# Last four attention units: heads and denominators placed from SBUF to SBUF, without the DRAM buffer

## The reference, cut to what matters

```python
q, k, v = (split_heads(holo_linear(x, ...)) for each of q, k, v)
attn = softmax(einsum('bhqd,bhkd->bhqk', q, k) * scale)
out = einsum('bhqk,bhkd->bhqd', attn, v)          # then back to [B, L, C]
x = _layernorm(x + holo_linear(out, basis_o, phase_o, amp_o))
logits = x @ router_w                              # the router of the experts
```

## Time and profile before

| | |
|---|---|
| median of 3 runs | 962.42 us (960.38 to 962.68) |
| the profiled execution, its own time | 961.26 us |
| its span in the profile | 959.6 us |
| PE busy | 757.4 us (79%) |
| DVE busy | 742.0 us (77%) |
| ACT busy | 470.8 us (49%) |
| mean granted clock of TensorE | 0.925 |

### The profile page before, as it was taken

How to read it: one execution, slowest core, us unless ns; L and a number is a source line. 1 busy time by engine, 2 the same in 40 slices (tenths; PEclk the granted TensorE clock), 3 DMA queues, 4 the chain that set the end, 5 groups by cost and what they waited for, 6 DMA issues and landing times.

```text
span 959.6 us, 12348 instructions
## 1 busy us (share of the span) xinstructions
PE 757.4 (79%) x3664; PEld 301.3 (31%) x3664; DVE 742.0 (77%) x1187; ACT 470.8 (49%) x550; POOL 395.6 (41%) x511
## 2 busy tenths in 40 slices
PE   5369999999999999988669983964667766678783
PEld 3212222222222222245547771321222222225211
DVE  3589999999999999666011225878999999998758
ACT  2237777777777777734213222784323323231452
POOL 3526533322333222005714543008987787570000
PEclk9659999999999999997979996956999989899997
DMA  5652122212222113120124413023544434420131
GB/s 125 203 210 53 53 54 56 53 49 53 55 53 57 50 53 93 44 59 26 52 59 125 120 55 99 3 91 132 198 157 149 153 129 162 147 88 1 44 74 58
DMA packets 57431, 83.79 MB, mean 87 GB/s; under 512 B 16211, under 2 KB 35078, under 8 KB 57382
## 3 DMA queue, kind: packets, MB, share of 16 engines
q1 hardware_dynamic: 44450, 66.19, 22.4%
q0 software_dynamic: 9472, 11.09, 4.0%
q10 hardware_dynamic: 3460, 5.89, 1.7%
HBM read 63.58 MB, written 16.16 MB: 83 GB/s over the span
## 4 chain that ended last, share of the span: by engine, by line
PE 39%; DVE 35%; issue 12%; POOL 5%; DMA 4%; ACT 3%; SPq 1%; DVEq 0%; ACTq 0%; POOLq 0%
DVE arena L1029 13%; PE pair L1436 10%; PE pair L1424 7%; PE pair L1519 7%; DVE arena L1288 7%; DVE arena L1282 5%; PE pair L1625 4%; PE pair L1614 4%; POOL slot_x_d L639 3%; POOL arena L703 1%; DVE xnum L283 1%; DVE ln_stats L271 1%; PE pair L1680 1%; DVE arena L1347 1%; DVE xT L1348 1%
## 5 line engine op out<-in xcount | busy, mean ns | idle before, releaser
L1029 DVE TENSOR_REDUCE arena<-pair 128x1 f32<-128x512 f32 x512 | 327.0, 685 | 20.2 <-PE pair L1426 16.8
L753 ACT ACTIVATE arena<-pair 128x1024 f32<-128x1024 f32 x256 | 248.2, 1021 | 94.9 <-PE pair L1436 94.8
L703 POOL TENSOR_TENSOR arena<-arena 128x1024 f32<-128x1024 f32 x64 | 149.9, 2355 | 47.8 <-DVE arena L1282 43.5
L1282 DVE TENSOR_TENSOR_SCAN arena<-pair,arena 128x1024 f32<-128x1024 f32 x64 | 145.7, 2277 | 2.6 <-POOL arena L703 2.6
L908 ACT ACTIVATE pair<-arena,alog 128x1024 f32<-128x1024 f32 x64 | 71.5, 1118 | 148.8 <-DVE arena L1282 148.8
L1519 PE MATMUL pair<-arena 128*32 128x512 f32 x1024 | 136.8, 606 | 0.6 <-ACT arena L753 0.6
L1738 PE MATMUL pair<-arena,ident 128*128 128x512 f32 x256 | 127.9, 624 | 11.7 <-DVE arena L1294 11.7
L1436 PE MATMUL pair<-arena 99*128 99x512 bf16 x512 | 134.8, 386 | 0.1
L1424 PE MATMUL pair<-arena 64*128 64x512 bf16 x256 | 102.8, 402 | 30.2 <-DVE arena L1029 22.6
L1426 PE MATMUL pair<-arena 64*128 64x512 bf16 x256 | 102.9, 402 | 0.0
L1729 PE MATMUL pair<-arena,sel 96*128 96x512 bf16 x128 | 40.6, 400 | 72.3 <-DVE arena L1288 66.3
(11 more groups left out here) (262 smaller groups left out, 953.5 us busy)
## 6 DMA issues: line engine op xcount, KB each, us to landing
arena<-b_rows_d SPq DMA_DIRECT2D x64, 512.0 KB, 3.6
arena<-in_L_ffn_w SPq DMA_DIRECT2D x16, 256.0 KB, 2.9
arena<-q_parts_d SPq DMA_DIRECT2D x32, 96.0 KB
arena<-q_parts_d POOLq DMA_DIRECT2D x32, 96.0 KB, 2.4
arena<-k_parts_d SPq DMA_DIRECT2D x32, 96.0 KB
arena<-xT SPq DMA_DIRECT2D x12, 256.0 KB
slot_x_d<-zero ACTq DMA_DIRECT2D x4, 645.0 KB, 8.9
arena<-slot_x_d SPq DMA_DIRECT2D x8, 322.5 KB, 4.1
```

The lines of the kernel that those rows point to most:

```text
L703: g.tensor_tensor(dBu[:, k % HRING, :], du[:, q, :], Bs[:, k % HRING, :], ALU.mult)\
L753: sc.activation(probs[:, kt % NPROB, :], st_pair[kt % 2][:, :], ACT.Exp, scale=SCALE)\
L1029: v.reduce_max(mx[:, mslot, n // 2, n % 2:n % 2 + 1], ring_bank[item % 3], AX).then_inc(s_("ring_read"), 1)
L1282: v.tensor_tensor_scan(hh[:, k % HRING, :], dA_pair[k % 2][:, :], dBu[:, k % HRING, :], 0.0, ALU.mult, ALU.add)\
```

## The change

For units 28 to 31 (`DIRECT = 4`) the DRAM tensor is no longer used. `place_rows` sends the 8 output rows of a group from `pvs` to their place in `o_par` with one DMA, and `place_den` sends its row of denominators to two partitions of `den` with two DMAs of 256 numbers. A unit therefore takes 12 DMAs (`place_head`) where it took 4 (`store_head`). In unit 31 SP and ACT issue six each, the four of denominators first. The denominators of the first 12 heads of batch 1 are loaded from DRAM in unit 29, with 8 DMAs (`load_some_dens`), behind the load of the first 12 heads. The two waits and the four loads after unit 31 are gone. The wait for the stores of the first 28 units moves ahead of the placing in unit 29, ACT's waits before it overwrites `pvs` in units 30 and 31 are for the placing, and DVE has two more waits ahead of the sum of the denominators.

```diff
+DIRECT = 4
+STORED = 4 * 16 * (UNITS - DIRECT) // 2 + 16
+PLACED = 12 * 16
...
+        def place_den(dma, u, s, g, signal):
+
+            head, par, qh = u % HEADS, g // 2, g % 2
+            at = 64 + 32 * qh + head
+            for k in range(2):
+                dma(den[at + 16 * k:at + 16 * k + 1, par, :],
+                    pvs[32 * g + HD:32 * g + HD + 1, s, k * (CH // 2):(k + 1) * (CH // 2)]).then_inc(s_(signal), 16)
+
+        def place_rows(dma, u, s, g, signal):
+
+            row, par, qh = u % HEADS * HD, g // 2, g % 2
+            dma(o_par[row:row + HD, par, L + qh * CH:L + (qh + 1) * CH], pvs[32 * g:32 * g + HD, s, :]).then_inc(s_(signal), 16)
...
+            def load_some_dens():
+                for par in range(2):
+                    for k in range(4):
+                        src = bass.AP(tensor=head_out_d.tensor, offset=((HEADS * 2 + par) * (HD + 1) + HD) * L + k * (L // 4),
+                                      ap=[[2 * (HD + 1) * L, HEADS - DIRECT], [1, L // 4]])
+                        sp.dma_start(den[64 + 16 * k:64 + 16 * k + HEADS - DIRECT, par, :], src).then_inc(s_("den_loaded1"), 16)
+
+            def place_head(u, s):
+
+                sp.wait_ge(s_("pv_copied"), u + 2)
+                for g in range(4):
+                    place_rows(sp.dma_start, u, s, g, f"head_stored{s}")
+                    place_den(sp.dma_start, u, s, g, f"head_stored{s}")
...
-                if not (first and s == 0):
+                if last and s == 1:
+                    for parity in range(2):
+                        sp.wait_ge(s_(f"head_stored{parity}"), STORED)
+                if last and s > 0:
+                    place_head(u - 1, (s - 1) % 2)
+                elif not (first and s == 0):
                     store_head(u - 1, (s - 1) % 2)
...
                 else:
-                    store_head(u, s % 2, range(1))
+                    sp.wait_ge(s_("pv_copied"), u + 2)
+                    for g in (0, 2):
+                        place_den(sp.dma_start, u, 1, g, "den_loaded1")
+                    for g in (0, 2):
+                        place_rows(sp.dma_start, u, 1, g, "o_loaded1")
                 if last and s == 1:
-
-                    for parity in range(2):
-                        sp.wait_ge(s_(f"head_stored{parity}"), 4 * 16 * (UNITS // 2 - 2) + 16)
-                    load_heads(HEADS, HEADS - 4, "o_loaded1")
+                    load_heads(HEADS, HEADS - DIRECT, "o_loaded1")
+                    load_some_dens()
...
-            for s in range(2):
-                sp.wait_ge(s_(f"head_stored{s}"), 4 * 16 * UNITS // 2 + 16)
-            load_dens(1, "den_loaded1")
-            load_heads(UNITS - 4, 4, "o_loaded1")
...
-                act.wait_ge(s_(f"head_stored{s % 2}"), 4 * 16 * (2 * i + s // 2) + 16)
+                if last and s >= 2:
+                    act.wait_ge(s_(f"head_stored{s % 2}"), STORED + PLACED)
+                else:
+                    act.wait_ge(s_(f"head_stored{s % 2}"), 4 * 16 * (2 * i + s // 2) + 16)
                 sc.copy(pvs[:, s % 2, :], pv_bank).then_inc(s_("pv_copied"), 1)
                 if last and s == 3:
                     act.wait_ge(s_("pv_copied"), UNITS + 1)
-                    for qh in range(2):
-                        dst = bass.AP(tensor=head_out_d.tensor, offset=(u * 2 + 1) * (HD + 1) * L + qh * CH,
-                                      ap=[[L, HD + 1], [1, CH]])
-                        act.dma_start(dst, pvs[64 + 32 * qh:64 + 32 * qh + HD + 1, 1, :]).then_inc(s_("head_stored1"), 16)
+                    for g in (1, 3):
+                        place_den(act.dma_start, u, 1, g, "den_loaded1")
+                    for g in (1, 3):
+                        place_rows(act.dma_start, u, 1, g, "o_loaded1")
...
-                dve.wait_ge(s_(dens), (4, 2)[b] * 16)
+                dve.wait_ge(s_(dens), (4, 16)[b] * 16)
+                if b == 1:
+                    dve.wait_ge(s_("head_stored0"), STORED + 2 * PLACED)
+                    dve.wait_ge(s_("head_stored1"), STORED + PLACED)
                 ch(v.tensor_tensor(den[rows, 0, :], den[rows, 0, :], den[rows, 1, :], ALU.add))
                 v.reciprocal(den[rows, 1, :], den[rows, 0, :]).then_inc(s_("recip_ready"), 1)
-                dve.wait_ge(s_(f"o_loaded{b}"), 4 * 16)
+                dve.wait_ge(s_(f"o_loaded{b}"), (4, 6)[b] * 16)
```

## The result

| | kernel before | changed kernel |
|---|---|---|
| median | 962.31 us (960.38 to 962.68, 4 runs) | 977.27 us (976.33 to 980.01, 4 runs) |
| ratio | | 1.0164, 95% interval 1.0147 to 1.018 |
| span of the profiled execution | 959.6 us | 976.3 us |
| mean granted clock | 0.925 | 0.914 |

The change costs 15 us. The forecast was +0.6, its range ended at 967.4.

The account below looks back on a forecast made before the run. Two paths to the projection behind unit 31 bound the kernel: heads from DRAM and ACT - norm - PE. 0 from part 3 and +0.57 from parts 1 and 2 gave 963.0 us against 962.42, range 960.6 to 967.4.

Parts of the forecast that it names:

- two paths that meet at the projection: Tail behind unit 31: heads from DRAM, and ACT - norm - PE, meet at the projection at 426.75 us.
- The room of PE's path: Tail, ahead of the projection: 1.24 us of room on ACT - norm - PE, the ceiling of the change's gain.
- The landing of `load_max`: Units 29 and 30: its data are there 2.1 us after its start, so PE does not stall.
- The landings of the placings: Unit 31: denominators there at 418.6 and last rows by 419.3, before DVE asks, so their landing is covered.
- fixed costs of DMAs overlap and issue time alone counts: ACT's six DMAs: four stores issue in 1.36 us, so issue time is counted, not about 2.0 us for each DMA.
- parts 2 and 3: ACT's six DMAs in unit 31 and SP's queue in units 29 and 30, priced by issue time.
- the third rival: SP's queue: denominator DMAs cost as `load_max`, 0.85 with the gap; +8.2 us, 970.6; chance 0.16.
- part 3: SP's queue, units 29 and 30: 12 DMAs take 4.96 us where 4 took 1.36; `load_max` in time, cost 0.
- Part 2: ACT's queue, unit 31: six DMAs take 2.76 us, table load 1.8 us later, projection +0.57 us.
- D: Delay of ACT's table load behind unit 31: 1.8 us, 1.3 to 3.4 with the bounds, undiminished through norm and logits.
- SP late: Units 29 and 30: dear denominator issues make `load_max` late; +8.2 us, or +4 at 0.6 an issue; chance 0.16.
- Clock: Tail: PE idles 2.4 us, its clock falls before the spread; +2 to +4, total +2.6 to +4.6, 966.0; chance 0.19.

Follow-up runs that it names:

- e3: Changed kernel with 30 extra matmuls in place of 14 behind unit 31: 975.49 us, ratio 1.0137 to the kernel before.
- e6: Changed kernel with only unit 31 placed from SBUF to SBUF, by SP and POOL; units 28 to 30 go by DRAM as before: 962.33 us, ratio 1.0002.
- e8: Kernel of e7 with 28 extra matmuls in place of 14: 964.64 us, ratio 1.0025 to the kernel before.
- e1: Changed kernel with load_max issued ahead of the 12 placings in units 29 and 30: 971.43 us, ratio 1.0089 to the kernel before.
- e2: Changed kernel with ACT's six DMAs of unit 31 issued by POOL: 970.2 us, ratio 1.0078 to the kernel before.
- e4: Kernel before with 32 unneeded DMAs of several forms, SBUF to SBUF or with DRAM on one side, added where SP's queue is idle: 961.33 us, one run.
- e7: Kernel before with four needless SBUF-to-SBUF DMAs of 8 rows on ACT's queue ahead of the table load: 969.25 us, ratio 1.0086.
- e5: Changed kernel with the edits of e1 and e2 together: 965.89 us, ratio 1.0048 to the kernel before.
- e10: Kernel before with 17 extra matmuls in place of 8 ahead of the turning of batch 1: 960.44 us, ratio 0.9993.

## Why the prediction was wrong

**What held.** The reading of what bounds the tail: two paths that meet at the projection, with the heads' trip from DRAM gone as a wait and ACT - norm - PE in its place. The room of PE's path, though it is 1.6 us (e3, e6, e8) and not 1.24: the prediction took the ends of the extra matmuls from the rows and added two handovers of 0.04, and in e6 the next matmuls start 0.08 and 0.16 ahead of those ends. The landing of `load_max`, 2.0 us against 2.1 (3.0 once, in e1). The landings of the placings, covered in e2 and e6. That fixed costs of DMAs overlap and issue time alone counts: it did, at 1.4 and 2.2 times the prices I took. (The 2.0 us that the prediction quotes from the Trainium skill, "DMA: Bandwidth & Descriptors", stand there in a section on DMAs issued from GpSimd; here they went from SP and ACT.)

**The step that failed: the price of an issue** in parts 2 and 3. "Eight rows of 512 are priced like a store, 0.33 with the gap" was 0.73; "I take 0.42" for the denominators was 0.58 to 0.62. I took the rows nearest by size and number of partitions, and these had DRAM on one side. For these forms the price goes by the two ends (e4). The trace of before held two lines with both ends in SBUF: `load_max` at 0.82, which I set aside because it changes the form, and the copies between halves of the channels late in the program, in equal form, 64 rows:

```profile
L486 SPq DMA_DIRECT2D arena<-xT x12: 461/572/599, 895.3 to 934.2; - x12
```

That row gives 0.57. I had it in hand before the prediction and left it out of the earlier trace rows, so that "the nearest SBUF-to-SBUF row is the dear one" in the third rival is false. With 0.62 for a denominator and 0.73 for the rows of a head, gaps included, part 3's own sum gives 7.9 us for twelve placings (7.7 measured) and a `load_max` that is 2.1 us late in unit 29 (1.9) and 5.2 in unit 30, the first delay within it (5.0). Part 2's sum gives 4 x 0.65 + 0.3 + 2 x 0.73 = 4.4 us on ACT's queue where 0.95 stood before, so D = 3.4; measured were 4.7 and D = 3.7, one of the two issues of rows having taken 1.26.

**The rivals** had the mechanisms. "SP late" named the place, the point from which it decides (0.45 for an issue) and +4 us at 0.6 an issue, still far too little: it priced the rows as a store in that case too. "Clock" named the fall ahead of the spread and +2 to +4; in the changed kernel the projection came 19.2 - 12.4 = 6.8 us later behind the copy, of which D - 1.6 = 2.2 is ACT's delay by the room that e3, e6 and e8 show, so the clock cost 4.6. The same sum gives 4.6 for the traces of e1 and e7. The second error was to give them chances as if they excluded each other. A late ACT is what makes PE idle, and the idling is what drops the clock: e7 shows four issues bringing both. One wrong price moved three terms at once (`load_max`, ACT's delay, the clock), and the range, built from cases taken one at a time, ended below their sum.

**Budget of the 15 us**, by medians: `load_max` late 5.8 with its two falls of the clock (e1); ACT's queue 7.1 with its fall (e2), 4 to 4.6 of it the clock (e3, e8); SP's queue in unit 31, which comes up when ACT's is mended, 3.6 more, by the step from e5 to e6. That step also takes the placings of units 28 to 30 back to DRAM, so the 3.6 is the worth of the whole step, and that it is DVE's wait of 2.76 us is argued from e5's trace. They sum to 16.5 for 15.0, with 1 to 2 us of uncertainty on each.

What stays open: why the placings of 8 rows cost 0.69 where e4's cost 0.62 to 0.65, what makes some loads from DRAM as dear as a placing, how often the tail of the kernel before loses its clock, and how much of e6's 2.6 us of shorter tail is left in the program's time.

## What to carry to other kernels

Price a DMA issue from a row with the same two ends and a like form: here from SBUF to SBUF it held the queue for about 0.6 us for 1 to 64 rows, twice the 0.3 of the stores to DRAM, so 12 small placings held SP's queue for 7.7 us where 4 stores had held it for 1.4. Before DMAs are added to a queue, list what stands behind them on it: a 6 KB transfer and a square root, both on the critical path, made up the loss, and an idle queue (POOL's) took the same six DMAs without delaying the tail. Where PE waits longer than before, add the fall of its clock to the delay, as one event and not as another case.

## What the runs showed of the hardware that was not expected

- An issue from SBUF to SBUF: 0.51 to 0.70 us on SP for 1 to 64 rows (first one 0.98), against 0.24 to 0.31 with DRAM on one side for 1 and 8 rows (e4), but 0.56 to 0.62 for 64 rows of 256 from DRAM (L379, before); on ACT 0.61 to 0.74 for a row in 16 pieces, and 0.67 and 1.26 for the two of 8 rows.
- A delay of 2.8 us of one square root cost 7.2 us of program time, of which 14 needless matmuls gave back 4.2 to 4.6 (e7, e8).
- "TensorE: Matmul & The Clock Gate" of the Trainium skill says in Part 1 that the clock halves after idling. The traces agree: 0.5 from 430 to 442 us behind 4.34 us of idling in the changed kernel, and 1.00 from the turning to the projection in the kernel before, which idled 0.60. But e10's trace, with the same 0.60, has 0.55 from 426 to 428, so how long PE idled ahead of the turning doesn't settle it alone.
- The kernel before itself runs from 958.5 to 966.5 us (0.8%) over the series, so 2 us won in a tail are hardly to be seen in ten runs (the interval of e6 is 1.7 us either way).
